# Full-width score matmuls, an adapter product in three parts, and two weight tiles side by side, in a one-core transformer block

## The reference

```python
# x (32, 64, 1024) f32; ids1 (32,) picks one of 32 adapters, ids2 (32,) one of 8 languages
def cond(x):                     # linear with a per-sequence rank-16 adapter
    h = einsum('bti,bir->btr', x, lora_As[ids1])
    return x @ W.T + b + 2.0 * einsum('btr,bro->bto', h, lora_Bs[ids1])
def attn(x):                     # 32 query heads, 8 key/value heads, head_dim 128, 64 tokens a sequence
    q, k, v = x @ wq, x @ wk, x @ wv        # then rope on q and k
    p = softmax(where(causal, q k^T / sqrt(128), -max))
    return (p v) @ wo
x = x + attn(cond(x))
x = x + ffn(cond2(x))            # two linears with routed adapters (top 2 of 8, top 2 of 16)
```

## Time and profile before

| | before |
|---|---|
| median of 3 runs | 2648.16 us (2645.89 to 2649.03) |
| the profiled execution | 2646.27 us |
| its span, first to last instruction | 2644.5 us |
| granted TensorE clock, mean | 0.997 |
| TensorE busy | 2602.4 us, 98% of the span |
| weight loads busy | 2094.4 us, 79% |
| VectorE / ScalarE / GpSimd busy | 51% / 32% / 39% |

### The profile page before, as it was taken

One profiled execution on the slowest core, in us unless ns is written; L12 is line 12 of the kernel. 1 busy time (PEld: TensorE's weight loads), 2 busy tenths in 40 slices (PEclk: granted clock), 3 DMA queues, 4 the chain that ended last, 5 costly groups with the idle time before them and its releaser, 6 DMA issues.

```text
span 2644.5 us, 35285 instructions
## 1 busy us (share of the span) xinstructions
PE 2602.4 (98%) x13448; PEld 2094.4 (79%) x13448; DVE 1338.2 (51%) x2035; ACT 833.9 (32%) x2066; POOL 1023.3 (39%) x670
## 2 busy tenths in 40 slices
PE   9999999999999999999999999999999999999999
PEld 7877777777776788888887787777777678888887
DVE  3236777777776111124623777777777511112452
ACT  2123344444444211211212334444444422121120
POOL 0034756666654533510303444333343443351030
PEclk9999999999999999999999999999999999999999
DMA  6422233333335523112543233333333451311232
GB/s 196 105 96 89 96 128 126 109 116 128 128 124 179 174 65 112 48 40 63 150 99 117 90 105 116 116 101 104 116 116 100 175 189 50 112 48 40 80 102 76
DMA packets 283065, 286.17 MB, mean 108 GB/s; under 512 B 47586, under 2 KB 225890, under 8 KB 282898
## 3 DMA queue, kind: packets, MB, share of 16 engines
q1 hardware_dynamic: 236034, 237.25, 28.6%
q10 hardware_dynamic: 46864, 46.67, 5.3%
HBM read 211.84 MB, written 72.02 MB: 107 GB/s over the span
## 4 chain that ended last, share of the span: by engine, by line
PE 90%; POOL 4%; DMA 2%; DVE 1%; SPq 1%; ACT 1%; issue 1%; POOLq 0%; ACTq 0%; DVEq 0%
PE prod L665 28%; PE prod L667 27%; PE prod L666 27%; PE turned L873 3%; PE turned L827 2%; POOL o_lo L1465 1%; POOL s_lo L1418 1%; PE turned L842 1%; PE prod L738 1%; DMA raw<-in_wo 1%; PE prod L697 1%; PE turned L857 0%; DMA raw_pair<-in_wq 0%; POOL w_lo L1398 0%; ACT probs L1188 0%
## 5 line engine op out<-in xcount | busy, mean ns | idle before, releaser
L1398 POOL TENSOR_TENSOR w_lo<-raw,w_hi 128x1024 fp32r<-128x1024 f32 x96 | 238.0, 2480 | 788.6 <-ACT w_hi L1079 788.3
L665 PE MATMUL prod<-o_hi,w_hi 128*128 128x512 f32 x1024 | 402.4, 393 | 13.6 <-POOL o_lo L1465 10.3
L667 PE MATMUL prod<-o_hi,w_lo 128*128 128x512 f32 x1024 | 398.6, 389 | 0.0
L666 PE MATMUL prod<-o_lo,w_hi 128*128 128x512 f32 x1024 | 398.6, 389 | 0.0
L1753 DVE TENSOR_TENSOR x<-prod,x 128x512 f32<-128x512 f32 x128 | 88.5, 692 | 561.7 <-PE prod L667 561.7
L1418 POOL TENSOR_TENSOR s_lo<-w_sum,s_hi 128x512 fp32r<-128x512 f32 x192 | 248.8, 1302 | 298.2 <-ACT s_hi L1156 298.2
L1079 ACT CAST w_hi<-raw 128x1024 fp32r<-128x1024 f32 x130 | 136.2, 1048 | 654.8 <-PE prod L667 527.9
L665 PE MATMUL prod<-t_hi,s_hi 128*128 128x512 f32 x768 | 311.7, 406 | 8.0 <-POOL s_lo L1418 8.0
L666 PE MATMUL prod<-t_lo,s_hi 128*128 128x512 f32 x768 | 301.0, 392 | 0.0
L667 PE MATMUL prod<-t_hi,s_lo 128*128 128x512 f32 x768 | 300.4, 391 | 0.0
L1418 POOL TENSOR_TENSOR s_lo<-raw_pair,s_hi 128x512 fp32r<-128x512 f32 x144 | 198.7, 1387 | 149.9 <-ACT s_hi L1156 146.0
(11 more groups left out here) (162 smaller groups left out, 4691.8 us busy)
## 6 DMA issues: line engine op xcount, KB each, us to landing
o_scratch<-o_out ACTq DMA_DIRECT2D x64, 512.0 KB, 3.1
raw<-in_wo SPq DMA_DIRECT2D x64, 512.0 KB, 4.1
o_raw<-o_scratch SPq DMA_DIRECT2D x64, 512.0 KB, 6.9
raw<-in_tw SPq DMA_DIRECT2D x50, 512.0 KB, 3.6
raw_pair<-in_wq SPq DMA_DIRECT2D x48, 512.0 KB, 3.8
w_sums_scratch<-w_sum SPq DMA_DIRECT2D x96, 256.0 KB, 4.4
w_sum<-w_sums_scratch SPq DMA_DIRECT2D x96, 256.0 KB, 4.5
xt_raw<-in_x SPq DMA_DIRECT2D x32, 256.0 KB, 5.7
```

What stands on the lines that cost most here:

```text
L665: pe.matmul(dst, wh, xh, start=start, stop=False)
L666: pe.matmul(dst, wh, xl, start=False, stop=False)
L667: return pe.matmul(dst, wl, xh, start=False, stop=stop)
L1398: pool.tensor_tensor(WL[i % 2][:], RAW[i % 2][:], WH[i % 2][:].bitcast(F32), ALU.subtract).then_inc(w_lo, 1)
```

## The change

- **Scores.** The two heads' rotated queries lie in one tile `Q[t]`, head by head within each sequence, so that 128 stationary columns hold both heads of a sequence. A unit is 8 matmuls of 128 stationary and 64 moving columns. The layouts of `VX`, `PT`, `pv`'s output and `o_out`'s copy follow. `pv` keeps its four matmuls of 256 columns, `turn_v` its transposes; VectorE adds v in one instruction per tile in place of two.
- **Adapter product.** `c_lora(n)` becomes `three`: high and low parts of `HM` and of each 128x128 block of `B1S` are made by ScalarE (`hm_high`, `b1_high`) and VectorE (`hm_low`, `b1_low`; in place, over `HM` and `B1S`). c_lora(0), (1) and (2) stand behind c_main(2). Tile 2's load is moved ahead of the adapter rows' loads on SP. The waits for the adapter rows move from TensorE to ScalarE.
- **wo's first two tiles.** For kb = 0 and j = 0, 1 the chunk loop holds both tiles: 6 matmuls a chunk. Order: (j 0, 1; t = 0), transposes and a score unit, (j 0, 1; t = 1), a score unit and transposes, then j = 2. The rest of the last head group's work and of its softmax moves with it.

```diff
@@ SP, start of a half
                 load_x(hf, 1)
+                load_w1(hf, 2)
                 for t in range(TT):
                     sp.wait_ge(out_done[t], hf * (16 * KC) + 16)
                 load_b1(hf, 0, slice(0, D))
-                for n in range(2, T_WO):
+                for n in range(3, T_WO):
@@ TensorE
                 def c_lora(n):
                     j, t = W1_ORDER[n]
-                    pe.matmul(PJ[QN[f"c{j}.{t}"] % 4][:], B1S[:, j * P:(j + 1) * P], HM[:, t * NT:(t + 1) * NT],
-                              start=False, stop=True).then_inc(prod, 1)
+                    pe.wait_ge(l_lo, lora_no(hf, n))
+                    hold(pe)
+                    three(PJ[QN[f"c{j}.{t}"] % 4][:], B1H[n % 2][:], B1L[:, j * P:(j + 1) * P], HMH[:],
+                          HML[:, t * NT:(t + 1) * NT], False, True).then_inc(prod, 1)
...
                 h_lora(0)
-                pe.wait_ge(taken, q_base + QN["h0"] + 1 + 4)
-                pe.wait_ge(b1_in, 16 * SPT * (3 * hf + 1))
-                hold(pe)
-                c_lora(0)
-                c_lora(1)
-                for n in range(2, T_WO):
+                c_main(2)
+                for n in range(3):
+                    c_lora(n)
+                for n in range(3, T_WO):
...
-                    for b in range(BPT):
-                        for r in range(2):
-                            for s in range(2):
-                                c = b * P + s * SEQ
-                                o = (b // 2) * 2 * P + r * P + (b % 2) * SEQ
-                                mm = pe.matmul(SCB[s * SEQ:(s + 1) * SEQ, o:o + SEQ],
-                                               Q[r][t][:, c:c + SEQ], K[:, t * NT + c:t * NT + c + SEQ],
-                                               start=True, stop=True)
+                    for s in range(SPT):
+                        mm = pe.matmul(SCB[:, s * SEQ:(s + 1) * SEQ], Q[t][:, s * P:(s + 1) * P],
+                                       K[:, t * NT + s * SEQ:t * NT + (s + 1) * SEQ], start=True, stop=True)
...
+                tile_ready(T_WO)
+                tile_ready(T_WO + 1)
+                for t in range(TT):
...
+                    for k in range(KC):
+                        if t == 1 and k >= 4:
+                            pe.wait_ge(o_lo_d, 4 * hf + k - 3)
+                        else:
+                            pe.wait_ge(o_lo, o_lo_at(hf, 0, t * KC + k))
+                        for j in range(2):
+                            ws = slice(k * P, (k + 1) * P)
+                            mm = three(PJ[wo_q(0, j, t) % 4][:], WH[j][:, ws], WL[j][:, ws], flat(OH[0], t)(k),
+                                       parts(o_lows(0), t)(k), k == 0, k == KC - 1)
...
+                    if t == 0:
+                        turn_p(last_gg, 0, 1)
+                        score(last_gg, 1, 0)
+                    else:
+                        score(last_gg, 1, 1)
+                        turn_p(last_gg, 1, 0)
@@ ScalarE (behind tile_hi(2), 4 casts of x, tile_hi(3), 4 casts of x)
+                def hm_high(t):
+                    act.wait_ge(taken, q_base + QN[f"h{t}"] + 1 + 4)
+                    if t:
+                        act.wait_ge(prod, q_base + QN["c7.0"] + 1)
+                    act.copy(HMH[:], HM[:, t * NT:(t + 1) * NT]).then_inc(l_hi, 1)
+                def b1_high(n):
+                    j, t = W1_ORDER[n]
+                    act.wait_ge(b1_in, 16 * SPT * (3 * hf + 1 + (0 if t == 0 else 1 + (j >= 4))))
+                    if n >= 2:
+                        pj, pt = W1_ORDER[n - 2]
+                        act.wait_ge(prod, q_base + QN[f"c{pj}.{pt}"] + 1)
...
+                    act.copy(B1H[n % 2][:], B1S[:, j * P:(j + 1) * P]).then_inc(l_hi, 1)
+                hm_high(0)
+                b1_high(0)
+                b1_high(1)
+                for n in range(KC):
                     c_hi(n)
-                    tile_hi(hf, n + 2, QN[f"c{n}.0"])
+                    if n >= 2:
+                        tile_hi(hf, n + 2, QN[f"c{n}.0"])
+                    if n + 2 < KC:
+                        b1_high(n + 2)
+                hm_high(1)
+                b1_high(KC)
+                b1_high(KC + 1)
@@ VectorE
                 h_mask(0)
+                hm_low(0)
+                b1_low(0)
+                b1_low(1)
                 for k in range(KC):
                     x_lo(hf, 1, k)
                 for j in range(KC):
...
                     dve.wait_ge(taken, c_raw(f"c{j}.0", j, CR[j][:]))
                     cb_low(name, j % 4, CR[j][:])
+                    if j + 2 < KC:
+                        b1_low(j + 2)
+                hm_low(1)
+                b1_low(KC)
+                b1_low(KC + 1)
```

More of the change, by code:

```diff
@@ L149, in build @@
         HM = sb("h_masked", [P, TT * NT], offset=188 * KB)
+        B1L = sb("b1_lo", [P, D], F32R, offset=184 * KB)
+        HML = sb("h_masked_lo", [P, TT * NT], F32R, offset=188 * KB)
         CE = [sb(f"c_even{i}", [P, NT], offset=(192 + 2 * i) * KB) for i in range(2)]
@@ L156, in build @@
         VX = [sb(f"v_rows{t}", [P, NT], offset=(116 + 2 * t) * KB) for t in range(TT)]
-        Q = [[sb(f"q_rot{r}{t}", [P, NT], offset=(122 + 4 * r + 2 * t) * KB) for t in range(TT)] for r in range(2)]
+        Q = [sb(f"q_rot{t}", [P, 2 * NT], offset=(122 + 4 * t) * KB) for t in range(TT)]
         K = sb("k_rot", [P, TOK], offset=130 * KB)
@@ L207, in build @@
         BA32 = sb("small_b2", [P, M_AF])
+        small_at = at[0]
         LG = sb("logits", [P, TB * EF])
         PR = sb("route_p", [P, TB * EF])
+        B1H = [sb(f"b1_hi{i}", [P, P], F32R, offset=small_at + 4 * P * i) for i in range(2)]
         GA = sb("gate_a", [P, TB * EF])
@@ L296, in build @@
         o_lo_d = sem("o_lo_dve")
+        l_hi = sem("lora_hi")
+        l_lo = sem("lora_lo")
         x1_hi = sem("x1_hi")
@@ L410, in wo_q, with wo_order @@
         def wo_q(kb, j, t):
+            if kb == 0 and j < 2:
+                return Q_WO + 2 * t + j
             return Q_WO + (kb * KC + j) * TT + t
+        def wo_order(kb):
+            jt = [(j, t) for j in range(KC) for t in range(TT)]
+            return [(0, 0), (1, 0), (0, 1), (1, 1)] + jt[4:] if kb == 0 else jt
         @block.sync
@@ L853, in turn_v @@
                     for t in range(TT):
[L854 to L857, removed]
+                        for b in range(BPT):
+                            o = t * NT + b * P
+                            mm = pe.transpose(TP[0][:, o:o + P], VX[t][:, b * P:(b + 1) * P], ident)
                     mm.then_inc(v_turned, 1)
@@ L867, in pv @@
                     hold(pe)
[L868 to L874, removed]
+                    n4 = GQ * SEQ
+                    for b in range(2):
+                        for s in range(2):
+                            rows = slice(s * SEQ, (s + 1) * SEQ)
+                            bb = 2 * hb + b
+                            mm = pe.matmul(OB[s][:, b * n4:(b + 1) * n4], VV[rows, t * NT + bb * P:t * NT + (bb + 1) * P],
+                                           PT[t][rows, bb * n4:(bb + 1) * n4], start=True, stop=True)
                     mm.then_inc(pv_done, 1)
@@ L1171, in _ @@
                         tile_hi(hf, n + 3, QN[f"c{j + 4}.1"])
+                        b1_high(n + 3)
                     for i, (name, src) in enumerate((("t1", CR[j]), ("t3", CE[0]), ("t2", CE[1]), ("t4", CR[j + 4]))):
@@ L1209, in o_out @@
                         act.wait_ge(o_stored, 16 * w)
-                    for b in range(2):
-                        ins = act.copy(view(OS_[:], GQ, b * P, (b + 1) * P), view(OB[b], GQ))
+                    for s in range(2):
+                        ins = act.copy(OS_[:].rearrange("p (h b s n) -> p b h s n", h=GQ, b=2, s=2)[:, :, :, s],
+                                       OB[s].rearrange("p (b h n) -> p b h n", b=2, h=GQ))
                     ins.then_inc(o_taken, 1)
@@ new lines, in _ @@
+                    for j, t in wo_order(kb):
+                        q = wo_q(kb, j, t)
+                        xs = slice(j * TOK + t * NT, j * TOK + (t + 1) * NT)
+                        is_prod(q)
+                        if kb == 0:
+                            dve.wait_ge(x1_in[j], 16 * (hf + 1))
+                        else:
+                            dve.wait_ge(taken, q_base + wo_q(kb - 1, j, t) + 1 + 4)
+                        dve.tensor_tensor(X1[:, xs], PJ[q % 4][:], X1[:, xs], ALU.add).then_inc(taken, 1)
+                        if kb == 0 and (j, t) == (1, 0):
+                            mask(last_v + 2)
+                            normalise(last_v + 2)
+                        if kb == 0 and (j, t) == (1, 1):
+                            mask(last_v + 3)
+                            normalise(last_v + 3)
+                        if kb == OKB - 1:
+                            dve.wait_ge(x1_hi, hf * (TT * KC) + TT * j + t + 1)
```

(2 more changed lines are left out.)

109 lines of the change are left out of this document (42 added, 67 removed).

## The result

The changed kernel takes 2674.58 us (median of 5 runs, 2671.72 to 2677.72) against 2647.10 for the kernel before, measured beside it (5 runs, 2645.89 to 2649.03): ratio 1.0105, 95% interval 1.009 to 1.0119. It is slower by 27.5 us; the forecast was 2673, from a sum of +25.3. The profiled execution is the longest of the five, 2677.72 us with a span of 2675.9 us, so differences read between the two traces add up to 31.4 us, not 27.5.

A forecast was written before the change was run, and what follows sets the result against it. TensorE, 98% busy, was taken to bound the kernel. Terms +32 - 4.3 + 4 + 6 - 12.4 = +25.3 on the profiled 2646.27 gave 2671.6; with medians 1.9 above that execution, the forecast was 2673 us, range 2654 to 2696.

The forecast's parts named there:

- Scores: 64 score units: 128-column weight loads set the pace, 1.78 us a unit in place of 1.28, +32 us.
- Adapter product: Three matmuls take 0.68 us in place of 0.87, -0.18 each; the 24 outside the halves' starts give -4.3 us.
- wait for tile 2: In wo, tile 2's cast and subtraction start only after the first j is done, leaving TensorE waiting 0.9 us.
- The first rival: Scores: loads hidden under the matmuls ahead, a unit falls to 1.06 us, total 2627 us, faster; 10%.
- Start of a half: Stage 1, n = 0 to 3: old waits go, new ones come, +2.2 us a half, +4 us for both.
- Both waits: At the start of each half, TensorE waits 1.9 us at c_lora(0) and 5.4 us at c_lora(2).
- n = 8 to 10: Stage 1's change of t: late adapter rows delay tile 10, a 2.0 us wait plus slow clock, +6 us for both halves.
- Stage 1 as a whole: Adapter products -4.3, the halves' starts +4 and the change of t +6 us; together +5.7 us.
- wo's pair: wo's first two tiles: 2.0 us lost in place of 8.2 in each half, -12.4 us for both.

The follow-up runs named there:

- wo_only: Kernel before the change with only the pairing of wo's first two weight tiles: 2635.59 us, ratio 0.9957.
- moving_128: Changed kernel with 128 moving columns in each score matmul in place of 64: 2671.65 us, ratio 1.0095 to the kernel before.
- order_by_half: Kernel before with each score unit's 16 matmuls reordered, all of one column half and then all of the other: 2690.26 us, ratio 1.016.
- adapter_only: Kernel before with only the split adapter product, its casts and subtractions, and tile 2's moved load: 2655.76 us, ratio 1.0033.
- scores_only: Kernel before with only the full-width scores, the turn_v and pv edits and the layouts they need: 2675.64 us, ratio 1.0111.
- after_fixed: Changed kernel with stage 1 reordered (tile 3's load, c_lora(2), b1_high(9), b1_low(2) and (3)): 2653.91 us, ratio 1.0027 to the kernel before.
- best: Changed kernel with stage 1 reordered and the scores of before in two column halves: 2622.52 us, ratio 0.9907 to the kernel before.
- all_but_scores: Changed kernel with the score unit, turn_v and pv of before: 2645.56 us, ratio 0.9992 to the kernel before.

## Why the prediction was right

**Scores.** The mechanism and the size held: a unit went from 1.28 to 1.79 us where 1.78 was forecast. 64 units of +0.51 are 32.7. In the changed kernel's trace 60 of them lengthen attention by 29.0 (30.6 by units), and the four inside wo add 1.0 rather than 2.0, since each half's wait for tile 2 is 0.86 where wo_only has 1.38. "TensorE has no slack, so all of this reaches the end" was a little too strong: the kernel before had one wait of 2.1 us in attention, with the clock at half behind it, and the changed kernel's list of waits no longer has it. The term of +32 is 30 in the trace, and 27.6, 29.0 and 31.4 in the three pairs of medians that differ by the scores alone. The first rival had the loads run under the matmuls ahead of them. They do, by moving_128; but a load of 128 columns is longer than the matmul of 64 that it runs under, so it still sets the pace. The Trainium skill's TensorE: Matmul & The Clock Gate, section LDWEIGHTS, has a load take its columns / 1.2 ns, an estimated 107 ns for 128 columns; 1.79 / 16 = 0.112 agrees. The Trainium skill's TensorEngine Tiling (Array Packing), section Performance Considerations, advises two column tiles for free dimensions of 64 or less; 1.28 against 1.79 agrees, and order_by_half adds that the gain hangs on neighbours going to different halves.

**Adapter product.** It takes 0.69 us in place of 0.87. Over n = 11 to 15 that gave -0.75 in each half, where 5 x 0.18 = 0.9 was forecast.

**Start of a half.** Both waits came, by the chain that was foreseen: 0.82 and 4.98 us in the first half and 1.49 and 4.98 in the second, in place of 1.9 and 5.4, with more than 2.9 us at 0.50 behind the longer one. The stretch is +2.2 and +2.5 in the table, +1.8 and +2.1 with the edge put right, against +2.2. Two errors of the forecast partly cancel: the waits were shorter, and the low clock lasted longer than the assumed 2.9 us, from 155.93 to about 159.1.

**n = 8 to 10.** The new wait is 1.59 and 2.08 us where 2.0 was forecast, and the slow clock came in one half of two. With the shorter products that is +0.7 and +2.8, 1.75 on the mean, as forecast. Stage 1 as a whole is +6.7 in this trace and +6.3 in that of adapter_only, where +5.7 was forecast.

**wo's pair.** 8.0 us lost became 2.1, and the wait for tile 2 is 0.86; the forecast had 8.2, 2.0 and 0.9. That wo_only's medians give exactly the -12.4 that was written is luck to the digit: its trace has -10.8, and the medians are uncertain by 4.

**What was not foreseen.** The prediction has nothing at tile 6 of wo. TensorE already waited there before the change, 1.66 and 1.68 us, with the clock whole behind it. In the changed kernel's profiled execution both halves lose 1.6 us between tile 6 and tile 7, behind waits of 1.82 and 2.22 and with the clock at half. Nothing was edited there, and it isn't a property of one of the parts: scores_only, adapter_only, after_fixed and best have the loss in one half, wo_only and all_but_scores in none. Why the clock falls there in some executions stays open; no run isolates it.

**The sum.** The terms follow their forecasts more loosely than 2673 against 2674.58 suggests. The profiled execution, the longest of five, is 31.4 longer than the one before, against a sum of 25.3: 3.2 of that is tile 6 and 1.7 the wait for the first tiles of the execution, and neither is in the forecast. The mechanism was right; agreement to 2 us is in part luck. Nor do the medians of the parts quite add up: 27.6 + 7.8 - 12.4 = 23.0 against 27.5 together. Each of these is uncertain by 3 to 4.5 us (half-widths of 0.0013 to 0.0017 in the ratios), so the 4.5 between them is within the noise, and no cause is claimed for it.

## What to carry to other kernels

Where few columns move and every matmul needs a new load, price a plain float32 matmul by its stationary columns: two 64-column halves in alternation beat one full-width instruction, though they are twice as many. When a product gets a new operand from a second engine, read that engine's queue from the operand backwards. A short cast or subtraction that stands behind eight ready subtractions, or one ahead of a cast that TensorE needs sooner, holds up TensorE for as long as they last, and another order of the same instructions takes it back (some 20 us here). Where a change bundles gains with a loss, test the parts alone: the 12 us of wo's pair were hidden under the scores, and the adapter product's gain came only with the other order.

## What was unexpected of the hardware

32, 64 and 128 moving columns behind a 128-column load cost the same to within 0.01 us a unit of 16. Narrow instructions all in one column half run 0.058 us from start to start, so a full-width instruction (0.112) costs about as much as two narrow ones in a row, and the alternation makes two narrow ones cost about one. The granted clock does not follow from the length of the last wait alone: at tile 6 of wo it fell to half behind a wait of 1.82 us in the changed kernel, and stayed whole behind the same 1.82 in after_fixed and behind 2.21 in all_but_scores. Each of the two falls in the changed kernel cost 1.6 us.
